# Step 0 of a graph attention block: ScalarE alternates three heads of exponentials with one copy of Q or K

## The reference

```
q, k, v = heads(x @ Wq + bq), heads(x @ Wk + bk), heads(x @ Wv + bv)   # 6 heads of 64
scores  = q @ k.T / sqrt(64) + where(adj, 0, -9e15)
probs   = softmax(scores)
y       = x + merge(probs @ v) @ Wf + bf
out     = (y - mean(y)) / sqrt(var(y) + 1e-5)
```

## Time and profile before

| what | value |
|---|---|
| runs | 1001.26 us median of 3 (1001.25 to 1001.6) |
| profiled execution | 1002.12 us, of which the span is 1000.3 us |
| PE | 991.7 us busy, 99% of the span |
| DVE | 706.7 us, 71% |
| POOL | 633.1 us, 63% |
| ACT | 589.5 us, 59% |

### The profile page before, as it was taken

One profiled execution on the slowest core, in us unless ns is written; L12 is line 12 of the kernel. 1 busy time (PEld: TensorE's weight loads), 2 busy tenths in 40 slices (PEclk: granted clock), 3 DMA queues, 4 the chain that ended last, 5 costly groups with the idle time before them and its releaser, 6 DMA issues.

```text
span 1000.3 us, 27877 instructions
## 1 busy us (share of the span) xinstructions
PE 991.7 (99%) x7690; PEld 900.2 (90%) x7690; DVE 706.7 (71%) x2760; ACT 589.5 (59%) x2130; POOL 633.1 (63%) x653
## 2 busy tenths in 40 slices
PE   9999999999999999999999999999999999999997
PEld 8788999889999889998899988999988999889997
DVE  5676766867668667677676686766777766867667
ACT  4766545675446665466654566554666545675556
POOL 2446657567566576575675765766656657567566
PEclk9999999999999999999999999999999999999999
DMA  8776676666776666766667666667666676665543
GB/s 186 175 196 167 172 210 189 178 163 171 199 193 186 168 170 175 218 172 182 161 176 204 188 178 169 173 183 207 181 173 168 171 215 181 176 171 160 160 151 104
DMA packets 344780, 178.08 MB, mean 178 GB/s; under 512 B 228784, under 2 KB 328752, under 8 KB 344752
## 3 DMA queue, kind: packets, MB, share of 16 engines
q1 hardware_dynamic: 343264, 176.77, 64.8%
q10 hardware_dynamic: 1488, 0.98, 0.3%
HBM read 103.35 MB, written 74.32 MB: 178 GB/s over the span
## 4 chain that ended last, share of the span: by engine, by line
PE 97%; ACT 1%; DVE 0%; DMA 0%; issue 0%; POOL 0%; SPq 0%; POOLq 0%; DVEq 0%
PE work_ps L427 16%; PE work_ps L429 15%; PE work_ps L428 15%; PE scores_ps L446 9%; PE scores_ps L466 9%; PE scores_ps L427 7%; PE scores_ps L429 7%; PE scores_ps L428 7%; PE work_ps L508 6%; PE scores_ps L508 6%; ACT probs L866 1%; DMA x_in<-in_x 0%; ACT qT L894 0%; PE scores_ps L545 0%; PE scores_ps L556 0%
## 5 line engine op out<-in xcount | busy, mean ns | idle before, releaser
L866 ACT ACTIVATE probs<-probs,neg_max 128x128 f32<-128x128 f32 x768 | 297.5, 392 | 87.9 <-DVE neg_max L676 87.9
L1038 POOL TENSOR_TENSOR probs<-probs,inv_sum 128x768 f32<-128x768 f32 x128 | 188.3, 1471 | 152.0 <-DVE inv_sum L699 152.0
L676 DVE CUSTOM_DVE_ANT_0 probs<-scores_ps,mask_bias 128x128 f32<-128x128 f32 x768 | 167.3, 286 | 127.9 <-PE scores_ps L446 127.2
L875 ACT COPY v_sb<-work_ps 128x384 f32<-128x384 f32 x128 | 61.3, 479 | 263.4 <-PE work_ps L429 263.4
L1033 POOL TENSOR_SCALAR y_sb<-y_sb,mean_var,rstd 128x384 f32<-128x384 f32 x120 | 198.4, 1653 | 21.5 <-POOL rstd L1023 21.5
L1023 POOL TENSOR_TENSOR rstd<-var_eps,minus_half 128x1 f32<-128x1 f32 x128 | 86.5, 676 | 168.5 <-DVE var_eps L720 168.5
L866 ACT ACTIVATION_READ_ACCUMULATOR probs<-probs,neg_max 128x1 f32 x768 | 146.9, 191 | 0.0
L1017 POOL TENSOR_TENSOR x_bias<-x_in,bias_row 128x384 f32<-128x384 f32 x128 | 128.9, 1008 | 7.7 <-DVE bias_row L829 7.7
L427 PE MATMUL scores_ps<-wf_hi,cT_hi 128*128 128x384 f32 x384 | 129.3, 337 | 0.0
L429 PE MATMUL scores_ps<-wf_hi,cT_lo 128*128 128x384 f32 x384 | 129.2, 336 | 0.0
L428 PE MATMUL scores_ps<-wf_lo,cT_hi 128*128 128x384 f32 x384 | 129.1, 336 | 0.0
(11 more groups left out here) (94 smaller groups left out, 2068.1 us busy)
## 6 DMA issues: line engine op xcount, KB each, us to landing
p_out<-p_turned SPq DMA_DIRECT2D x125, 384.0 KB, 2.8
pT<-p_out SPq DMA_DIRECT2D x500, 96.0 KB, 2.8
x_in<-in_x SPq DMA_DIRECT2D x128, 192.0 KB, 2.9
x_blocks<-in_x SPq DMA_DIRECT2D x372, 64.0 KB, 2.3
out<-y_sb SPq DMA_DIRECT2D x120, 192.0 KB, 2.1
adj_u<-in_adj SPq DMA_DIRECT2D x32, 64.0 KB, 2.1
out<-xT SPq DMA_DIRECT2D x4, 192.0 KB, 2.7
out<-qT SPq DMA_DIRECT2D x4, 192.0 KB, 1.9
```

The lines of the kernel that those rows point to most:

```text
L676: last = nc.vector.tensor_tensor_reduce(out=probs[:, e, h, :], in0=scores_ps[:, score_cols(e, h)], in1=mask_bias[:, e, :], scale=-SCALE, s ...
L866: last = nc.scalar.activation(probs[:, e, h, :], probs[:, e, h, :], ACT.Exp, bias=neg_max[:, e, h:h + 1], scale=-1.0, accum_out=row_sum[:, ...
L1038: nc.gpsimd.tensor_tensor(probs[:, e, :, :], probs[:, e, :, :], inv_sum[:, e, :].unsqueeze(2).broadcast_to([P, HEADS, SEQ]), ALU.mult).the ...
```

## The change

Only ScalarE's list in step 0 changes. `halved(g + 1)` is false only there; in every other step the list stays as it was. Before, step 0 made six exponentials (batch 0), copy 0, six exponentials (batch 1), copy 1, eight exponentials (batch 2 and two heads of batch 3), copy 2, the last four exponentials, then copies 3, 4 and 5. Now it makes three exponentials and one copy in turn, six times, and the six exponentials of batch 3 behind the last copy.

```diff
             def step(i, c):
 
                 g, n = TURN * i + c, first_of(i, c)
-                for e in range(HALVED):
-                    exps(e, n + e)
-                    if halved(g + 1):
+                if not halved(g + 1):
+                    for q in range(NJ):
+                        exps(q // 2, n + q // 2, q % 2 * MATS, (q % 2 + 1) * MATS)
+                        copy_qk(i, c + 1, q)
+                    exps(3, n + 3)
+                else:
+                    for e in range(HALVED):
+                        exps(e, n + e)
                         copy_half(i, c + 1, e)
-                    else:
-                        copy_qk(i, c + 1, e)
-                exps(2, n + 2)
-                exps(3, n + 3, end=2)
-                copy_qk(i, c + 1, 2)
-                exps(3, n + 3, first=2)
-                for half in range(2):
-                    copy_qk(i, c + 1, 3 + half)
...
+                    exps(2, n + 2)
+                    exps(3, n + 3, end=2)
+                    copy_qk(i, c + 1, 2)
+                    exps(3, n + 3, first=2)
+                    for half in range(2):
+                        copy_qk(i, c + 1, 3 + half)
...
```

More of the change, by code:

```diff
@@ L899, in step @@
                 g, n = TURN * i + c, first_of(i, c)
-                for e in range(HALVED):
-                    exps(e, n + e)
-                    if halved(g + 1):
-                        copy_half(i, c + 1, e)
-                    else:
-                        copy_qk(i, c + 1, e)
-                exps(2, n + 2)
-                exps(3, n + 3, end=2)
-                copy_qk(i, c + 1, 2)
-                exps(3, n + 3, first=2)
-                for half in range(2):
-                    copy_qk(i, c + 1, 3 + half)
[L912 to L915, removed]
+                if not halved(g + 1):
[6 more added lines that the diff above has]
+                        exps(e, n + e)
+                        copy_half(i, c + 1, e)
+                    exps(2, n + 2)
[4 more added lines that the diff above has]
+                        copy_qk(i, c + 1, 3 + half)
+                        if real(g - 1):
+                            for e in (2 * half, 2 * half + 1):
+                                round_ctx(e, n - GROUP + e)
+                    copy_qk(i, c + 1, 5)
                 if real(g + 2):
```

## The result

| | kernel before | changed kernel |
|---|---|---|
| median, 22 runs each | 1001.62 us (1001.19 to 1002.28) | 1003.3 us (1001.65 to 1004.21) |
| profiled execution | 1002.12 us, span 1000.3 | 1004.21 us, span 1002.4 |

The ratio is 1.0014, 95% interval 1.0007 to 1.002. The change costs 1.7 us by the medians and 1.4 us by the ratio. That is less than the 0.2% that the prediction called measurable, but the interval excludes "nothing", and 1003.3 lies outside the range of 1001.1 to 1002.7. The forecast was +0.45, to 1001.7. Of the 1.6 us between 1001.7 and 1003.3, 0.36 is not the change's: the forecast stood on three runs of the kernel before with a median of 1001.26, and 22 runs have 1001.62.

What follows compares the result with a forecast made beforehand. TensorE, busy 99% of the span, was taken as the bound. The terms -1.84 up to v0, +2.21 for v2's wait and +0.08 for its restart gave +0.45 us, to 1001.7; range 1001.1 to 1002.7.

Steps and rivals of the forecast that it cites:

- the removed waits: Step 0, TensorE: p3 and p4 no longer wait for ScalarE's copies, so v0 begins 1.84 us earlier.
- the added price: Step 0: six exponentials delay V copy 0, so v2 waits 2.2 us and comes out 0.37 later; restart 0.08 more.
- rival C: Step 0: the 2.2 us stop before v2 halves TensorE's clock, costing 3 to 6 us, 1004.7 to 1007.9; chance 3%.
- the turned probabilities: Step 1: batch 3's probabilities return through DRAM at 60.1, before its context product at 60.44; costed at nothing.
- rival B: Step 1: turned probabilities too late, batch 3's context product waits up to 1.2 us more, 1002.1 to 1002.9; chance 20%.
- The chain: SyncE's queue through DRAM runs 3.88 us later: store 3 issued at 51.57, last load landed at 60.1.
- The cover of 0.3: Step 1: 0.3 us left between the last load's landing and batch 3's context product; costed at nothing.

Runs made afterwards that it cites:

- E2: The changed kernel with no edit, run for a second profile; 1003.47 us, ratio 1.0017.
- E10: The changed kernel with only step 1's context product of batch 3 moved behind Q/K product p2; 1003.74 us, ratio 1.0019.
- E5: The changed kernel with eight unread transposes on TensorE between v1 and v2 of step 0; 1002.49 us, ratio 1.0009.
- E9: The changed kernel with eight transposes before v2 in step 0, and step 1's context product of batch 3 behind p2; 1002.52 us, ratio 1.0009.
- E6: The kernel before, with two more exponentials ahead of copy 2 in step 0, lengthening the stop before p4; 1003.78 us, ratio 1.0018.
- E3: The changed kernel with SyncE's four last x-block loads of step 0 behind the loads of the turned probabilities; 1002.78 us, ratio 1.0016.
- E7: The changed kernel with V copies 0 and 1 of step 0 ahead of the four roundings; 1002.12 us, ratio 1.0015.
- E8: The changed kernel with V copies 0 and 1 first, and four x-block loads between batch 2's and batch 3's loads; 1002.79 us, ratio 1.001.
- E11: The changed kernel with V copies 0 and 1 ahead of the roundings, and step 1's context product of batch 3 behind p2; 1002.15 us, ratio 1.0007.
- E12: The changed kernel with V copies 0 and 1 first and VectorE turning blocks 1 and 2 one inversion earlier in step 0; 1001.09 us, ratio 0.9993.
- E4: The changed kernel with 7 warm-up transposes in place of 4 between the first and second transpose of x; 1003.22 us.

## Why the prediction was wrong

**Right: the removed waits.** p0 to p5 ran in one piece. Counted from the scores of group 0, v0 came at 15.27 in place of 17.15, 1.88 us earlier (forecast 1.84), and counted from copy 0 it is within 0.05 of the forecast place (10.00 against 10.05). One small reading was off: p3 had begun 0.08 late in the kernel before, not 0.12 (p2's last matmul at 36.17, p3 at 36.48); the sum does not use it.

**Right: the added price.** The six exponentials before the roundings and the V copies turn this gain into a stop before v2. Forecast 2.2 and a net of +0.45, measured 2.04 and +0.37 (23.92 against 23.55).

**Wrong: what a stop of 2 us costs (rival C, 3%).** This is the step that failed: the sum took v2's wait at its length (+2.21, and 0.08 for the restart), and what the clock does behind it at nothing. The prediction's remark that "the rows here show no fall after 1.33 us and none for a stop of 2.2" was read as if it made the fall unlikely. The trace of before held no stop of that length and could not say. Nor can the row of nines in the earlier trace rows show such a fall: a slice is 25 us, a fall of 3.4 us leaves its mean at 0.93, and the page of E2, which has the fall, prints the same row:

```profile
PEclk9999999999999999999999999999999999999999
```

(For the kernel before the reading was right all the same: half a microsecond at a time, its clock is 1.00 from 39 to 55 us.) The fall occurs in 9 to 17 of the 33 executions and costs 1.54 us by the two profiles of the changed kernel (step 0 of 25.46 against 23.92). Shown by the two profiles with the clock at 0.50 (E2, E10), by filling the stop (E5, and E9 against E10: upper group gone), and by making the same stop in the kernel before (E6, upper group there). My price for it, 3 to 6 us, was too high as well: I had let it last through v2, v3 and the scores, and it ended before the scores.

**Mis-sized: the turned probabilities (rival B, 20%).** The chain was right to 0.01 us at the store of blocks 3, but the two landings behind it were taken from one row each (4.7 and 2.3; measured 3.6 and 3.6). The cover of 0.3 was then set to a cost of nothing. Profiles without a fall lose 0.3 to 0.8 (31.02, 30.97, 31.46 against 30.68). E9 could not take this term out alone, since the move costs 0.4 to 0.5 itself; so its share in the medians is read from the profiles, not shown by a difference of times.

Put together: without a fall 1001.6 + 0.37 + 0.3 to 0.8 = 1002.3 to 1002.8; with a fall 1001.6 + 0.37 + 1.54 = 1003.5. The median of all lies in the upper group since 13 of the 22 runs do, most of them by a fall and some (3 of the 13 have a clock of 0.999) without one. The range held the lower group but not the upper; it had left out a case that came in a quarter to a half of the executions.

**Open.** What decides in which execution the clock falls. Why the second x transfer lands late in some, and whether that makes all of the upper runs at 0.999; no other of them was profiled. What makes the upper runs of E3, E7, E8 and E11 (up to 1005.37), whose profiles show neither. And how short a stop is safe: E7 and E8, with no stop above 1.33 in their profiles, still have two runs of 0.997 each, while E11 and E12 (0.51 and 0.82) have none.

## What to carry to other kernels

Removing a wait of the bounding engine is only half of a reordering: follow the moved work until the next thing that this engine needs from the same queue, here a copy 1.64 + 2.33 us further down. Ask not only how much idle time TensorE has but how it is cut: one stop of 2 us cost up to 1.5 us more than its length, while stops of 1.2 to 1.4 did not in any profile. A clock row over slices of 25 us cannot show this; ask for the stretch itself. And a cover of 0.3 us over a chain of DMA transfers is no cover: the same store took 4.7 us to land in one profile and 3.6 in the other, the same load 2.3 and 3.6. Such a term needs a price of its own, not zero.

## What the runs showed of the hardware

- A stop of TensorE of 2.04 to 2.10 us was followed by a fall of the granted clock to 0.50 for 3.4 us in two of six profiles with such a stop (E2 and E10; not the first one, E3, E4 or E6). Behind stops of 1.17 to 1.36 (both profiles of before, E5, E7, E9) none was seen in a profile.
- A transpose of 128x128 took 0.24 us in the start and 0.13 in E5 (eight in 1.03), where the clock was at its upper level.
- Two more changes between the context product's form (128x128 through 64 columns) and the 128x512 form cost 0.34 us together in E9 (0.09 + 0.14 + 0.11 at the three places); its step 1 as a whole took 0.50 more, without a wait.
- From the scores of group 2 on, 912.99 us of matmuls took the same time to 0.01 us in fourteen profiles. All variation between these executions lies in the first 84 us; behind the start of the last matmul they differ by less than 0.1.
